# Slot-key turns and the flag's sum placed later in a graph-network kernel, and the ring positions folded behind the flag

## The reference

```python
src_h = h[src] @ W_msg.T + b_msg
emb = edge_embed[jnp.clip(edge_type, 0, NUM_EDGE_TYPES)]
messages = jax.ops.segment_sum(src_h + emb, dst, num_segments=num_nodes)
h_new = _gru_cell(messages, h[:num_nodes], W_ih, W_hh, b_ih, b_hh)
x = _layernorm(x + jnp.zeros_like(h).at[:num_nodes].set(h_new))
```

## Time and profile before

| | |
|---|---|
| median of 3 runs | 1030.27 us (1030.04 to 1030.69) |
| profiled execution | 1030.4 us |
| its span | 1028.5 us |
| mean granted clock of TensorE | 0.972 |
| PE, DVE, ACT, POOL busy | 92%, 82%, 61%, 74% of the span |
| last unit's cast starts (line 1162) | 64.74 us |
| group 0 starts on TensorE | 69.64 us |
| last gather starts on POOL | 1007.79 us |

### The profile page before, as it was taken

The page is one execution under the profiler, slowest core; times in us unless marked ns, Lnnn a source line. Parts: engine busy times, 40 slices in busy tenths (PEclk is TensorE's granted clock), DMA queues, the critical chain, the costliest instruction groups (busy, mean ns, idle before and its releaser), DMA issues.

```text
span 1028.5 us, 23000 instructions
## 1 busy us (share of the span) xinstructions
PE 941.9 (92%) x8241; PEld 621.8 (60%) x8241; DVE 844.2 (82%) x2678; ACT 625.3 (61%) x1207; POOL 762.4 (74%) x807
## 2 busy tenths in 40 slices
PE   5789899999999999999999999999999999999963
PEld 2256566666666656666666666666666666666641
DVE  8788888897989979987899788888888988886463
ACT  4664257665676567656676666767676667566231
POOL 7777777777777777777777777777777777777771
PEclk9888999999999999999999999999999999999986
DMA  8889223333334333334343433434343433343441
GB/s 268 232 248 303 55 63 89 94 97 93 106 85 111 94 97 103 103 93 110 80 108 99 111 94 96 109 96 110 97 109 93 112 94 105 101 112 99 106 128 43
DMA packets 95666, 116.98 MB, mean 114 GB/s; under 512 B 20027, under 2 KB 81271, under 8 KB 95544
## 3 DMA queue, kind: packets, MB, share of 16 engines
q0 software_dynamic: 36608, 75.94, 28.0%
q1 hardware_dynamic: 57080, 37.80, 12.5%
q10 hardware_dynamic: 1856, 1.68, 0.5%
HBM read 99.34 MB, written 16.00 MB: 112 GB/s over the span
## 4 chain that ended last, share of the span: by engine, by line
PE 66%; DVE 9%; ACT 7%; POOL 7%; issue 6%; DMA 4%; POOLq 0%; DVEq 0%; ACTq 0%; SPq 0%
PE psf L1114 30%; PE psb L1099 13%; POOL xg L604 7%; PE pAB L1042 5%; PE pAB L1056 5%; PE psg L1081 5%; ACT mem L1226 3%; DMA arena<-in_x 2%; PE psg L1077 2%; PE psg L1085 2%; PE pAB L1059 2%; DVE ohk L877 2%; DVE ohl L883 1%; ACT L1213 1%; DVE ohk L880 1%
## 5 line engine op out<-in xcount | busy, mean ns | idle before, releaser
L604 POOL DMA_INDIRECT xg<-x_split,idx x676 | 642.9, 951 | 206.0 <-issue 195.6
L1114 PE MATMUL psf<-mem 128*128 128x384 bf16 x2548 | 562.0, 327 | 7.4 <-ACT arena L1236 6.6
L1226 ACT CAST mem<-psb 128x432 f16<-128x432 f32 x832 | 400.3, 522 | 222.2 <-PE psb L1099 210.8
L1099 PE MATMUL psb<-ohk,ohl 128*128 128x108 bf16 (+3 forms) x1801 | 385.7, 258 | 17.4 <-ACT mem L1226 16.6
L877 DVE TENSOR_TENSOR ohk<-table_bank,prm 128x392 bf16<-128x392 f16 (+3 forms) x421 | 260.6, 619 | 64.1 <-PE psb L1099 61.8
L1114 PEld LDWEIGHTS psf<-mem 128*128 128x128 f16 x2548 | 219.3, 98 | 107.2 <-issue 18.9
L1099 PEld LDWEIGHTS psb<-ohk,ohl 128*128 128x128 bf16 x1801 | 165.9, 99 | 138.4 <-ACT mem L1226 31.1
L883 DVE TENSOR_TENSOR ohl<-table_bank,prm 128x512 bf16<-128x512 f16 x421 | 174.4, 414 | 0.0
L1081 PE MATMUL psg<-ohs,xg 128*128 128x56 bf16 (+9 forms) x2028 | 97.1, 196 | 12.7 <-DMA xg<-x_split,idx 8.5
L604 POOL DMA_INDIRECT xg<-in_x,idx x88 | 85.8, 975 | 29.6 <-issue 24.4
L1081 PEld LDWEIGHTS psg<-ohs,xg 128*128 128x128 bf16 x2028 | 86.4, 97 | 30.6 <-DMA xg<-x_split,idx 9.8
(11 more groups left out here) (148 smaller groups left out, 799.3 us busy)
## 6 DMA issues: line engine op xcount, KB each, us to landing
xg<-x_split,idx POOLq DMA_INDIRECT x676
x_split<-mem SPq DMA_DIRECT2D x24, 384.0 KB
xb<-in_xT SPq DMA_DIRECT2D x49, 128.0 KB
arena<-in_x SPq DMA_DIRECT2D x24, 256.0 KB, 7.2
arena<-in_xN SPq DMA_DIRECT2D x47, 128.0 KB
out<-arena SPq DMA_DIRECT2D x18, 128.0 KB
out<-spill SPq DMA_DIRECT2D x17, 128.0 KB
out<-spill SPq DMA_DIRECT2D x112, 8.0 KB
```

Source lines behind the costliest of these rows:

```text
L604: pool.indirect_dma_start(out=xg[:, p % RING, :] if split else xg32(p % RING), out_offset=None, in_=x_d if split else x, in_offset=bass.In ...
L1099: ins = pe.matmul(psb[:, bank % NB, held * HC:(held + m) * HC], ohl[:, e % KB, :], ohk[:, e % KB, d * HC:(d + m) * HC], start=(k == 0), st ...
L1114: pe.matmul(psf[:, 0:3 * H], Bb[q % 2][0:kk, HT + h, :], xs[0:kk, h, :, :].rearrange("p c f -> p (c f)"), start=(h == 0), stop=(h == HI - ...
L1226: act.copy(Bb[q % 2][:, :, n:n + MOST], psb[:, bank % NB, 0:MOST * HC].rearrange("p (d h) -> p h d", h=HC)).then_inc(S["s_eb"], 1)
```

## The change

`TURN_AT` becomes (20, 24): turns 0 and 1 stand behind steps 20 and 24 of the split on TensorE and ScalarE. Turns 2 and 3 stand behind the whole split on TensorE, ahead of its read of the flag. The flag's sum moves from step 19 to step 24, behind turn 1. The fold of the ring positions moves on VectorE from between the second and third piece of the keys to behind the flag, ahead of its copies of turns 2 and 3. No instruction is added or removed.

```diff
-TURN_AT = (15, 18, 21, 22)
+TURN_AT = (20, 24)
 BY_ACT = 2
-SUM_AT = 19
+SUM_AT = 24
...
             dense_keys(1)
-            over = chk[:, 0:GROUPS]
-            fold = 1 << ((N - ND) // R).bit_length() - 1
-            while fold:
-                link(v.tensor_scalar(over, g0, float(ND + fold * R), float(fold * R), ALU.is_ge, ALU.mult))
-                link(v.tensor_tensor(g0, g0, over, ALU.subtract))
-                fold //= 2
-            more(v.tensor_scalar(gbI[:, :], g0, float(ND), None, ALU.subtract))
             v.wait_ge(S["s_em"], 16 * 2)
...
             v.tensor_scalar(flag[:, :], vi[:, 4:5], 100.0, None, ALU.min).then_inc(S["s_fl"], 1)
+            over = chk[:, 0:GROUPS]
+            fold = 1 << ((N - ND) // R).bit_length() - 1
+            while fold:
+                link(v.tensor_scalar(over, g0, float(ND + fold * R), float(fold * R), ALU.is_ge, ALU.mult))
+                link(v.tensor_tensor(g0, g0, over, ALU.subtract))
+                fold //= 2
+            more(v.tensor_scalar(gbI[:, :], g0, float(ND), None, ALU.subtract))
             for a in range(BY_ACT, len(TURNS)):
...
                     pe.matmul(psg[0:1, 2 * P:2 * P + J + 2], one[:, :], badc, start=True, stop=True,
                               skip_group_check=True).then_inc(S["s_sum"], 1)
+            for a in range(BY_ACT, len(TURNS)):
+                turn(a)
             pe.wait_ge(S["s_fl"], 1)
...
-                if t in TURN_AT[:BY_ACT]:
+                if t in TURN_AT:
                     turned(TURN_AT.index(t))
```

## The result

| | kernel before | changed kernel |
|---|---|---|
| median, us (executions) | 1029.97 (7) | 1032.69 (7) |
| lowest to highest, us | 1028.83 to 1030.69 | 1029.58 to 1033.91 |
| profiled execution, its span, us | 1030.4, 1028.5 | 1029.58, 1027.7 |
| PE, DVE, ACT, POOL busy | 92, 82, 61, 74% | 91, 82, 61, 74% |
| TensorE's mean granted clock | 0.972 | 0.974 |

The ratio of the times, changed to before, is 1.0024, with a 95% interval of 1.0014 to 1.0034: slower by 2.5 us, 1.4 to 3.5 us. The forecast was 4.5 us and 1034.8 us. The profiled execution of the changed kernel is its shortest, 3.1 us under its median, and even 0.8 us shorter than the profiled one of before. So the two first traces do not show the loss. They show where group 0's time comes from; how much of it is an execution's luck had to come from more traces.

What follows compares the result with a forecast made beforehand. POOL's back-to-back gathers bound the kernel, so group 0's delay moves the end: last cast 2.5 us earlier (62.2 us) plus 11.4 us puts group 0 4.0 us later; with 0.5 us of clock, +4.5 us, 1034.8 us; range 1031.6 to 1037.0 us.

Steps and rivals of the forecast that it cites:

- POOL as the bound: Loop from gather 17: POOL issues gathers back to back, 746 steps of 1.2552 us, plus a fixed tail of 20.7 us.
- The rival that VectorE bounds the loop: Loop: its pace hangs on VectorE, so one-hots 5.9 us later reach the end, 1036.2 us; chance 0.10.
- VectorE's line behind the last cast: From the last unit's cast to group 0: flag, fold, copies, branch and one-hots in a line, 11.4 us.
- the 0.5 us of the sum: Group 0's matmuls on TensorE: the lower clock, 1.2 GHz, was taken to add 0.5 us.
- What comes ahead of that is unchanged: ScalarE in the split: all ahead of the end of step 15's round, at 45.6 us, stays as before.
- Least: no half-clock wait: Lower bound: no half-clock wait, no turn 0 wait, group 0 at 2.4 GHz take off 2.5 + 0.5 us, leaving +1.5 us.
- the 1.7 us of half-clock wait: ScalarE at unit 16: wanted at 47.5 us but ready at 49.2 us, as TensorE's clock is at half.
- The base of the sum: Start of the loop: the profiled execution before, with gather 17 at 71.42 us, to which the change's +4.5 us was added.
- the prediction's own sign of being wrong: Gather 17 starting by 71.4 us or earlier, among the signs given that the prediction is wrong.
- The rival "Faster": Split: its stalls are what counts, so gather 17 starts up to 2.73 us earlier, 1027.5 us at best; chance 0.04.
- was hidden, because VectorE was early: Fold at its old place on VectorE: its 3.07 us were hidden before the change.
- it frees 3.07 us there, [...] but nothing waits for that piece: VectorE ahead of the keys' third piece: moving the fold frees 3.07 us, unneeded with the sum at step 24.

## Why the prediction was right or wrong

It said slower by 0.44%, in a range of 1031.6 to 1037.0 us; measured were 0.24% and 1032.69 us. The direction was right, and so was the mechanism behind the last unit's cast; the place of that cast was wrong, and the size came out too large.

- **POOL as the bound** was right. All six traces have 936.4 to 939.5 us from gather 17 to the last, and the largest wait of POOL behind 100 us is its own gap. But neither length is fixed, as the sum had it: the tail behind the last gather was 19.8 to 20.7 us. The rival that VectorE bounds the loop is not borne out: group 0's one-hots came 1.4 us later in the changed kernel's first trace (69.04 against 67.63 us) and gather 17 only 0.07 us, the last gather 0.06 us, since it is group 0's end that counts. The Trainium skill, Perfetto Trace Analysis, section Identifying the Most-Contended Engine, calls the engine with the highest occupancy the most contended one, which among VectorE, ScalarE and POOL is VectorE here. The traces do not agree: behind 100 us POOL, 74% busy, waits only its own gap, while VectorE waits 60.6 us for line 1099's results between 100 and 950 us of before's first trace. No run made POOL's step itself shorter.
- **VectorE's line behind the last cast** was right to 0.6 us: 11.4 us forecast, 10.8 to 11.5 us measured, with the fold (3.0 us), the copies (4.5 us) and the lower clock in group 0 as worked out. In all three traces of the changed kernel VectorE's one-hots release group 0, so VectorE does take TensorE's place. The eight matmuls of group 0 took 1.91 to 1.92 us in all three, against 1.35, 1.06 and 1.06 us in the traces of before: the lower clock costs 0.56 to 0.85 us, not just the 0.5 us of the sum.
- **"What comes ahead of that is unchanged" and "Least: no half-clock wait"** was the step that failed. The last unit's cast was put at 62.2 us, and even without its waits at 59.7 us; it came at 57.4 to 58.6 us. I anchored ScalarE's rounds at the end of step 15, 45.6 us, in a trace in which unit 15's load was late. In the changed kernel's first trace unit 15's cast starts at 41.50 us instead of 44.13 us, 2.6 us earlier, and the clock is at its upper level, 2.4 GHz, from 44 to 50 us, so the 1.7 us of half-clock wait is gone too. Together that is the missing 4.2 us. Neither need be an effect of the change: unit 15's load is issued ahead of all that it moves, and before's second trace had the upper level as well.
- **What held turn 0** I had not named. A gain of the change is a wait for the keys (2.78 us in the third trace of before) that the late load hid in the first. It appears in my sum only as ScalarE's wait of 1.82 us.
- **The base of the sum** was late as well: gather 17 at 71.42 us is the latest of the three traces of before (69.38 and 70.74 us), 0.9 us above their mean.
- **That the time fell within the range is in part luck.** Gather 17 was put at 75.9 us and came at 71.49, 72.36 and 70.53 us, 4.4 us earlier on average; a start by 71.4 us or earlier was the prediction's own sign of being wrong, and the third trace shows it. With the base 0.9 us too late, the traces leave a difference 3.5 us smaller than the forecast 4.5 us. The runs leave one 2.0 us smaller. The 1.5 us in between helped the forecast, and nothing in its working accounts for them.
- **The rival "Faster"** asked for the last unit's cast at 58.2 us, and two of three traces had it (57.97 and 57.39 us). The kernel was still slower in every comparison. In the first of these traces group 0 started 0.5 us earlier than in before's first, but took 2.07 us at the lower clock against 1.51 us, and so ended 0.07 us later.
- **The fold "was hidden, because VectorE was early"** was right for before, and that "it frees 3.07 us there, [...] but nothing waits for that piece" as well: VectorE's idle ahead of the last records grew to 2.13, 3.28 and 2.78 us.

What stays open: the mean of gather 17 over three traces of each is 70.5 and 71.5 us, 1.0 us apart, while the medians are 2 to 3 us apart; and the profiled executions of both take the same time on average (1030.3 and 1030.2 us). Three executions of each are too few for spreads of 2 to 5 us, so the split of the 2.5 us between fold (0.7 us by trace, 1.5 us by medians) and turns is not settled closer than that. The experiments show which edits cost time and where their waits lie; that gather 17 alone carries the 2.5 us of the changed kernel is not shown.

## What to carry to other kernels

Look first for the engine that never waits, whatever its busy share, then for the one place where it does: here only POOL's first full ring connected 70 us of prologue with a millisecond of loop. Before you anchor a sum on a point of one trace, ask what would hold that point if the wait in front of it were missing; a late load can hide a wait for something else, and a second trace of the same kernel shows it. Work that stands in a wait for a DMA is free there and can cost time behind the last wait: here 0.7 us (by trace) of the 3.0 us of the moved fold, and nearly all of a second fold in the same place. So move work only if you know what it will stand in line with.

## What the runs showed of the hardware that I had not expected

- The same kernel's executions spread by 5.6 us (1026.84 to 1032.42 us in 23 runs on one chip), and the medians of the kernel before on three chips were 1028.79, 1031.71 and 1028.77 us.
- The 746 steps from gather 17 to the last took 936.37, 939.52 and 937.25 us in the three traces of before: up to 3.2 us from the pace of the indirect DMAs alone, more than the change itself costs. One gather of the prologue kept POOL 3.09 us in before's first trace, against 0.94 us for most.
- A load of x was waited for up to 4.10 us by ScalarE in one execution and not at all at the same place in another, and the last key records landed anywhere from 52.8 to 54.8 us.
- TensorE's granted clock fell to its lower level (1.2 GHz) at different places in traces of one kernel. In before it read 0.52 in the stretch 44 to 50 us of the first trace, behind a wait of 3.74 us, and 1.00 there in the second, behind a wait of 3.94 us. In the changed kernel it read 0.50 in the stretch 56 to 58 us of the second trace and 1.00 there in the first and third.
